# Target attention over a history: both halves of the next pair's scores ahead of the context, and one history transfer per group

## The chip, the cores and the metric

The kernel runs on one core of a Trainium2 chip. The metric is the device time of one execution in microseconds (us); the reference numbers are a median over runs. The engines are named as the profile names them: PE (TensorE matmuls) with PEld (its weight loads), DVE (VectorE), ACT (ScalarE), POOL (GpSimd) and SP (SyncE, which issues most DMAs; SPq is its queue).

## The reference, cut to what matters

For each of 2048 targets there is a history of 200 rows of 128 numbers and a mask of 200 flags. One query per target attends to its own history with four heads of 32.

```python
q = (target_item @ W_q).reshape(b, H, HD)            # b=2048, H=4, HD=32
k = (history_sequence @ W_k).reshape(b, S, H, HD)    # S=200
v = (history_sequence @ W_v).reshape(b, S, H, HD)
scores = jnp.einsum('bhd,bshd->bhs', q, k) / SCALE
scores = jnp.where(mask[:, None, :] == 0, NEG, scores)
attn = jax.nn.softmax(scores, axis=-1)
out = jnp.einsum('bhs,bshd->bhd', attn, v).reshape(b, A)
return out @ W_o
```

All data are float32. The history is 2048 x 200 x 128 x 4 bytes, 209.7 MB, and is read once. The kernel never forms k and v. It multiplies each target by W_q and W_k combined (four vectors `u` of 128 per target), takes the scores as `u` times the history, the context as the softmax weights times the history, and multiplies the context by W_v and W_o combined.

## The kernel before

**Tiling.** 16 targets make a *group*: their history fills one tile `hist[g % 6]` of 128 partitions (16 targets x 8) by 25 x 128 numbers. Two groups, i = 0 and 1, make a *pair* `p`; there are 64 pairs. Three pairs (96 targets) make a *round*, in which the targets are transposed (`transpose_target`), combined with the weights (`combine`) and the finished contexts are multiplied out (`outputs`). There are six history tiles, that is three pairs (RING = 3).

**One pair's way through the engines.** SP loads the history tile in two halves of 12 and 13 of its 25 slices (HALVES), and the mask. DVE transposes each half in 32 x 32 blocks into `blocks` (`turn`, four per pair; three `blocks` tiles exist). POOL spreads `u` into the padded weight tile `u_pad` (`spread`, 16 small copies) and turns the mask into `bias` (`mask_bias`). PE makes the scores of group 0 and of group 1 (`scores(p, 0)`, `scores(p, 1)`) into one PSUM bank `ps_s`. DVE adds the bias and takes the extreme (`maximum`), ACT takes the exponential (`exponent`), DVE divides and transposes (`turn_probs`, up to `probs_t`). PE places these weights (`place`, into `ps_p`), ACT expands them into `p_pad` with eight activations (`expand`), and PE multiplies them with the history (`context`, into two banks `ps_c`). ACT copies the context out (`finish`, to `ctx_sb`), PE transposes it while adding partial sums (`turn_context`, into `ps_y`), and ACT stores it in `ctx_t` (`copy_context`).

**Order.** Nothing is scheduled by a tool: each engine has its own program, written out by hand, and runs it in order, with semaphore waits between engines. The PE program is a sequence of `step(q)`, one for each pair, three to a turn of the loop. In step q the order is: `place(q)`, `scores(q+1, 0)`, wait for `expand(q)`, `turn_context` of pair q-1, `context(q)` of the first 12 slices of both groups, `scores(q+1, 1)`, `context(q)` of the other 13 slices. Where q is a multiple of three, `transpose_target` and `outputs` stand behind the first context half and `combine` behind `scores(q+1, 1)`. The DVE program for each pair p is `turn(p,0,0)`, `maximum(p-1)`, `turn(p,0,1)`, `turn_probs(p-1)`, `turn(p,1,0)`, `turn(p,1,1)`. The ACT program is `exponent(q)`, `finish(q-1)`, `expand(q)`, `copy_context(q-1)`, and in every third step the copies of the round (`copy_target`, `store`, `copy_combined`).

**When buffers come free.** A half of a history tile is loaded again once the context that reads this half for the pair three before has ended (L150). There is one `u_sb`, so that `copy_combined` waits until POOL has spread the last pair of the round before (L376). POOL's `mask_bias(p+2)` stands ahead of `spread(p+2)`, and waits for the mask that SP issued behind the first group's history of that pair.

**Start.** Behind the weight products PE makes 96 idle transposes (IDLE_TURNS), then the first scores.

## Time and profile before

| | |
|---|---|
| median of 3 runs | 766.93 us (765.03 to 769.29) |
| profiled execution, its own time | 765.87 us |
| span of the profiled execution | 764.1 us |
| PE / PEld / DVE busy | 76% / 59% / 68% of the span |
| ACT / POOL busy | 37% / 40% of the span |
| DMA queue of SP | 217.60 MB, 80.1% of 16 engines' span |
| mean DMA rate | 287 GB/s |

The span runs from the first to the last recorded instruction; the execution's own time is 1.8 us longer. A busy share is an average over the span, so no engine is at 100% although the work of one pair follows that of the other without a break. The rows quoted below carry, in order, the start in us, the duration in us, the engine, the line of the kernel, the operation with its tiles, the number of instructions merged into the row, and in brackets the idle time before it with what ended it.

### The profile page before, as it was taken

How to read it: one execution, taken by the hardware profiler on the slowest of the kernel's cores; microseconds unless marked ns; L12 is line 12 of the kernel's file. 1: busy time of each engine (PE TensorE's matmuls, PEld its weight loads, DVE VectorE, ACT ScalarE, POOL GpSimd, SP SyncE). 2: the span in 40 equal slices, each digit the busy share in tenths (PEclk: the TensorE clock that was granted, in tenths of full speed). 3: DMA queues.
4: the chain of work that ended last, by engine and by line, in shares of the span. 5: the costliest groups of instructions: out<-in, count | busy, mean ns of one | idle time of the engine just before them, and what ended most of it. 6: DMA issues, size and time to landing. Idle time of an engine off the chain costs nothing.

```text
span 764.1 us, 41709 instructions
## 1 busy us (share of the span) xinstructions
PE 578.2 (76%) x18665; PEld 449.7 (59%) x18665; DVE 520.7 (68%) x577; ACT 280.0 (37%) x909; POOL 305.7 (40%) x1123
## 2 busy tenths in 40 slices
PE   6877777777787777778777777878767777877776
PEld 5655665556566565556556555656656555655655
DVE  4475767776866767876776777686676777677660
ACT  2142334334433433433333433443343443343342
POOL 3624343453443344344344334344434434534420
PEclk9999999999999999999999999999999999999998
DMA  8578688788889788798978879898988979897940
GB/s 339 213 260 296 247 315 297 287 316 303 312 285 334 261 289 324 279 337 293 328 265 316 309 275 313 299 330 289 330 270 286 329 278 334 279 324 266 318 143 6
DMA packets 49808, 219.18 MB, mean 287 GB/s; under 512 B 5888, under 2 KB 16656, under 8 KB 49760
## 3 DMA queue, kind: packets, MB, share of 16 engines
q1 hardware_dynamic: 49056, 217.60, 80.1%
q0 software_dynamic: 704, 1.05, 0.4%
q8 instruction: 17, 0.28, 0.1%
q14 instruction: 31, 0.25, 0.1%
HBM read 217.58 MB, written 1.05 MB: 286 GB/s over the span
## 4 chain that ended last, share of the span: by engine, by line
PE 41%; ACT 17%; DVE 14%; DMA 10%; issue 9%; POOL 7%; SPq 1%; POOLq 0%; DVEq 0%; ACTq 0%
ACT p_pad L391 16%; PE ps_c L287 15%; PE ps_s L256 11%; DMA mask<-r_mask 10%; DVE blocks L456 8%; PE ps_p L270 7%; POOL u_pad L200 6%; PE ps_y L297 4%; DVE probs_t L480 3%; DVE weights L476 2%; PE ps_p L349 2%; POOL bias L204 1%; PE ps_y L304 1%; ACT probs L382 1%; DMA w_in<-L_rec_W_o 1%
## 5 line engine op out<-in xcount | busy, mean ns | idle before, releaser
L456 DVE STREAM_TRANSPOSE blocks<-hist 128x1536 f32<-128x1536 f32 (+1 forms) x256 | 454.4, 1812 | 6.4 <-DMA hist<-r_history_sequence 6.4
L200 POOL COPY u_pad<-u_sb 32x32 f32<-32x32 f32 x1024 | 233.6, 228 | 60.6
L287 PE MATMUL ps_c<-hist,p_pad 64*32 64x128 f32 x12800 | 221.4, 274 | 5.3 <-issue 4.8
L391 ACT ACTIVATE p_pad<-ps_p,own 128x200 f32<-128x200 f32 x512 | 169.7, 442 | 116.1 <-PE ps_p L270 116.1
L204 POOL TENSOR_SCALAR bias<-mask 128x200 f32<-128x200 int32 x64 | 56.4, 881 | 371.5 <-DMA mask<-r_mask 369.8
L256 PE MATMUL ps_s<-blocks,u_pad 128*32 128x200 f32 x4096 | 202.0, 338 | 0.0
L287 PEld LDWEIGHTS ps_c<-hist,p_pad 64*32 64x32 f32 x12800 | 185.3, 106 | 26.7 <-issue 19.4
L465 DVE CUSTOM_DVE_ANT_0 neg_score<-ps_s,bias 128x200 f32<-128x200 f32 x64 | 23.4, 366 | 198.9 <-PE ps_s L256 198.9
L256 PEld LDWEIGHTS ps_s<-blocks,u_pad 128*32 128x32 f32 x4096 | 121.0, 110 | 52.2 <-issue 8.8
L270 PE MATMUL ps_p<-probs_t,place_sel 128*64 128x112 f32 x1024 | 65.2, 271 | 82.8 <-DVE probs_t L480 82.8
L270 PEld LDWEIGHTS ps_p<-probs_t,place_sel 128*64 128x64 f32 x1024 | 51.3, 140 | 100.1 <-DVE probs_t L480 71.6
L297 PE MATMUL ps_y<-par_sel,ctx_sb 128*128 128x64 f32 x256 | 42.3, 288 | 84.5 <-ACT p_pad L391 84.0
L297 PEld LDWEIGHTS ps_y<-par_sel,ctx_sb 128*128 128x128 f32 x256 | 33.8, 192 | 109.1 <-issue 102.0
L382 ACT ACTIVATE probs<-neg_score,neg_max 128x200 f32<-128x200 f32 x64 | 29.6, 463 | 145.5 <-DVE neg_max L465 145.5
L406 ACT COPY ctx_t<-ps_y 128x128 f32<-128x128 f32 x64 | 25.4, 397 | 52.8 <-PE ps_y L297 52.8
L400 ACT COPY ctx_sb<-ps_c 128x128 f32<-128x128 f32 x128 | 27.6, 268 | 46.2 <-PE ps_c L287 46.1
L377 ACT COPY u_sb<-ps_u 128x384 f32<-128x384 f32 x22 | 10.5, 479 | 67.8 <-POOL u_pad L200 47.6
L480 DVE STREAM_TRANSPOSE probs_t<-weights 128x224 f32<-128x224 f32 x64 | 26.3, 411 | 2.9 <-DVE weights L476 0.2
L245 PE MATMUL ps_u<-x_t,w_qk 128*128 128x96 f32 x176 | 25.8, 291 | 2.8 <-issue 1.9
L245 PEld LDWEIGHTS ps_u<-x_t,w_qk 128*128 128x128 f32 x176 | 22.1, 197 | 9.8 <-issue 8.7
L304 PE MATMUL ps_y<-w_vo,ctx_t 128*96 128x128 f32 x176 | 23.1, 274 | 0.5 <-ACT ctx_t L406 0.5
L476 DVE TENSOR_SCALAR weights<-probs,inv_sum 128x200 f32<-128x200 f32 x64 | 20.9, 327 | 2.3
(42 smaller groups left out, 122.3 us busy)
## 6 DMA issues: line engine op xcount, KB each, us to landing
hist<-r_history_sequence SPq DMA_DIRECT2D x128, 832.0 KB, 7.9
hist<-r_history_sequence SPq DMA_DIRECT2D x128, 768.0 KB, 6.6
mask<-r_mask SPq DMA_DIRECT2D x64, 100.0 KB, 5.1
x_sb<-r_target_item SPq DMA_DIRECT2D x21, 48.0 KB, 9.0
out<-out_sb POOLq DMA_DIRECT2D x21, 48.0 KB, 4.5
w_in<-L_rec_W_q SPq DMA_DIRECT2D x1, 64.0 KB, 1.8
w_in<-L_rec_W_k SPq DMA_DIRECT2D x1, 64.0 KB, 2.2
w_in<-L_rec_W_v SPq DMA_DIRECT2D x1, 64.0 KB, 5.2
```

The source lines that it names most:

```text
L200: pool.tensor_copy(to, source[Q * c:Q * c + Q, a]).then_inc(u_pad_ready, 1)
L204: pool.tensor_scalar(bias[p % 2][:, :], mask_sb[p % RING][:, :], 0.0, BIG, ALU.is_equal, ALU.mult).then_inc(bias_ready, 1)
L245: mm = pe.matmul(ps_u[:, h * ROUND:(h + 1) * ROUND], w_qk[:, h, :], x_t[:, :], start=True, stop=True)
L256: mm = pe.matmul(ps_s[ring][Q * b:Q * b + Q, 0:S].rearrange("p (t j) -> p t j", j=J), u_pad[ring][:, i, b, c, :], blocks[slot][:, :, c, J ...
L270: mm = pe.matmul(ps_p[64 * alpha:64 * alpha + 64, 0:4 * TQ * 16].rearrange("p (q x i r) -> p x q i r", q=TQ, x=4, i=2)[:, x], place_sel[:, ...
L287: mm = pe.matmul(ps_c[alpha][at:at + Q, 0:D], p_pad[ring][rows, t + par, i, :], hist[2 * ring + i][rows, t + par, :], start=(t == 0), stop ...
L297: mm = pe.matmul(ps_y[:, 64 * alpha:64 * alpha + 64], ctx_sb[:, alpha, :], par_sel[:, :, :].rearrange("p i r -> p (i r)"), start=True, sto ...
L382: act.activation(probs[p % 2][:, :], neg_score[p % 2][:, :], ACT.Exp, bias=neg_max[:, 0:1], scale=-1.0, accum_out=row_sum[p % 2][:, 0:1]). ...
L391: op = act.activation(p_pad[p % RING][:, :, :, H * k:H * k + H].rearrange("p t i h -> p (t i) h"), source[:, k // 4], ACT.Copy, scale=own[ ...
L456: dve.transpose(blocks[g % BLOCKS][:, t0:t1].rearrange("p t c k -> p (t c k)"), hist[g % SLOTS][:, t0:t1, :].rearrange("p t d -> p (t d)") ...
L476: dve.tensor_scalar(weights[:, 0:S], probs[p % 2][:, :], inv_sum[:, 0:1], None, ALU.mult).then_inc(weighted, 1)
L480: dve.transpose(probs_t[:, :, :].rearrange("p q r -> p (q r)"), weights[:, :]).then_inc(probs_turned, 1)
```

## The change

Six things change together.

1. PE's step: both `scores(q+1, 0)` and `scores(q+1, 1)` stand right behind `place(q)`, ahead of the wait for `expand(q)`. The pieces of the round stand between the two scores, one for each step of the round: `transpose_target` where q mod 3 is 2, `combine` where it is 0, `outputs` where it is 1.
2. The context runs group by group, all 25 slices of group 0 and then of group 1, four slices side by side in the array in place of two slices of both groups. `ps_c` holds 2 x 128 columns, `finish` copies 256 columns for each bank, and `turn_context` makes four matmuls of 32 columns against `share_sel` in place of two of 64 against `par_sel`.
3. History is loaded in one transfer of 25 slices per group, once the context of the group six before has ended. DVE's two `turn`s of a group wait for that one transfer.
4. The mask of pair p+1 is issued behind the first history transfer of pair p. On POOL `spread(p+2)` stands ahead of `mask_bias(p+2)`, which waits for `maximum(p)` in place of `exponent(p)`.
5. `u_sb` is double, so that `copy_combined` waits for the spread of one round earlier. `outputs` writes into the `ps_u` bank.
6. IDLE_TURNS is 63 in place of 96.

```diff
-    IDLE_TURNS = 96
+    IDLE_TURNS = 63
...
-                    for h, (t0, t1) in enumerate(HALVES):
-
-                        wait(sp, ctx_done, 2 * (p - RING) + h + 1)
-                        sp.dma_start(
-                            hist[g % SLOTS][:, t0:t1, :], history_v[g * P:(g + 1) * P, t0:t1, :],
-                        ).then_inc(hist_loaded[g % SLOTS][h], 16)
...
+                    wait(sp, ctx_done, g - SLOTS + 1)
+                    sp.dma_start(hist[g % SLOTS][:, :, :],
+                                 history_v[g * P:(g + 1) * P, :, :]).then_inc(hist_loaded[g % SLOTS], 16)
+                    if i == 0 and p == 0:
+                        load_mask(0)
+                    if i == 0 and p + 1 < NP:
+                        load_mask(p + 1)
...
             for p in range(NP):
                 if p + 2 < NP:
-                    pool.wait_ge(exp_done, p + 1)
-                    pool.wait_ge(u_pad_ready, 16 * p + 32)
+                    pool.wait_ge(bias_ready, p + 2)
+                    spread(p + 2)
+                    pool.wait_ge(u_pad_ready, 16 * p + 48)
+
+                    pool.wait_ge(max_ready, p + 1)
                     mask_bias(p + 2)
-                    pool.wait_ge(bias_ready, p + 3)
-                    spread(p + 2)
...
-            def context(ring, half):
-                t0, t1 = HALVES[half]
-                for t in range(t0, t1, 2):
+            def context(ring, i):
+
+                for t in range(0, T, 4):
                     for alpha in range(2):
                         rows = slice(64 * alpha, 64 * alpha + 64)
-                        for i in range(2):
-                            for par in range(min(2, t1 - t)):
-                                at = Q * (2 * i + par)
-                                mm = pe.matmul(
-                                    ps_c[alpha][at:at + Q, 0:D],
-                                    p_pad[ring][rows, t + par, i, :],
-                                    hist[2 * ring + i][rows, t + par, :],
-                                    start=(t == 0), stop=(t + par + 2 >= T),
-                                )
+                        for x in range(min(4, T - t)):
+                            mm = pe.matmul(
+                                ps_c[alpha][Q * x:Q * x + Q, i * D:(i + 1) * D],
+                                p_pad[ring][rows, t + x, i, :],
+                                hist[2 * ring + i][rows, t + x, :],
+                                start=(t == 0), stop=(t + x + 4 >= T),
+                            )
                 mm.then_inc(ctx_done, 1)
 
             def turn_context():
                 for alpha in range(2):
-                    mm = pe.matmul(ps_y[:, 64 * alpha:64 * alpha + 64], ctx_sb[:, alpha, :],
-                                   par_sel[:, :, :].rearrange("p i r -> p (i r)"), start=True, stop=True)
+                    for i in range(2):
+                        at = 64 * alpha + Q * i
+                        mm = pe.matmul(ps_y[:, at:at + Q], ctx_sb[:, alpha, i, :], share_sel[:, :],
+                                       start=True, stop=True)
                 mm.then_inc(ctx_t_done, 1)
...
+            def step(q, ring, r, first=False, ahead=True, targets=True):
+
                 place(q)
                 if ahead:
-                    scores(q + 1, after, 0)
+                    scores(q + 1, (ring + 1) % RING, 0)
+                if targets and (ring == 2 or first):
+                    transpose_target(r + 2 if ring == 2 else 1)
+                if targets and ring == 0 and not first:
+                    combine(r + 1)
+                if ring == 1 and not (isinstance(r, int) and r == 0):
+                    outputs(q - 1)
+                if ahead:
+                    scores(q + 1, (ring + 1) % RING, 1)
                 pe.wait_ge(expanded, q + 1)
                 if not first:
                     pe.wait_ge(ctx_copied, 2 * q)
                     turn_context()
                 context(ring, 0)
...
-                wait(act, u_pad_ready, 16 * RING * r)
-                act.copy(u_sb[:, :, :], ps_u[:, 0:H * ROUND].rearrange("p (h n) -> p h n", h=H)).then_inc(u_copied, 1)
+                wait(act, u_pad_ready, 16 * RING * (r - 1))
+                act.copy(u_sb[r % 2][:, :, :], ps_u[:, 0:H * ROUND].rearrange("p (h n) -> p h n", h=H)).then_inc(u_copied, 1)
...
-                dve.wait_ge(hist_loaded[g % SLOTS][half], 16 * (g // SLOTS + 1))
+                dve.wait_ge(hist_loaded[g % SLOTS], 16 * (g // SLOTS + 1))
```

The first place is PE's program inside the loop, one step without and (after the change) one step with a piece of the round. `ps_s` are the scores, `ps_p` the placed weights, `ps_y` the turned context, `ps_c` the context; ISA and REGISTER_ALU rows set up loop counts. Before:

```order
L270 MATMUL ps_p<-probs_t,place_sel 64x7x16 x8
L250 ISA
L252 ISA
L256 MATMUL ps_s<-blocks,u_pad 32x200 x16
L316 REGISTER_ALU
L297 MATMUL ps_y<-par_sel,ctx_sb 128x64 x2
L287 MATMUL ps_c<-hist,p_pad 32x128 x48
L250 REGISTER_ALU
L256 MATMUL ps_s<-blocks,u_pad 32x200 x16
L287 MATMUL ps_c<-hist,p_pad 32x128 x52
```

After the change, in a step that holds `combine`:

```order
L273 MATMUL ps_p<-probs_t,place_sel 64x7x16 x8
L253 ISA
L255 ISA
L259 MATMUL ps_s<-blocks,u_pad 32x200 x16
L248 MATMUL ps_u<-x_t,w_qk 128x96 x4
L253 REGISTER_ALU
L259 MATMUL ps_s<-blocks,u_pad 32x200 x16
L326 REGISTER_ALU
L300 MATMUL ps_y<-share_sel,ctx_sb 128x32 x4
L288 MATMUL ps_c<-hist,p_pad 32x128 x100
```

The second scores moved from between the two context halves to ahead of the register row that carries the wait for the expanded weights; the piece of the round moved in between the two scores.

The second place is SP's queue in the steady part, over one pair. Before:

```order
L151 DMA hist<-r_history_sequence 128x1536 [waits ctx_done]
L151 DMA hist<-r_history_sequence 128x1664 [waits ctx_done]
L157 DMA mask<-r_mask 128x1x200 [waits bias_ready]
L151 DMA hist<-r_history_sequence 128x1536 [waits ctx_done]
L151 DMA hist<-r_history_sequence 128x1664 [waits ctx_done]
```

After the change:

```order
L157 DMA hist<-r_history_sequence 128x3200 [waits ctx_done]
L149 DMA mask<-r_mask 128x1x200 [waits bias_ready]
L157 DMA hist<-r_history_sequence 128x3200 [waits ctx_done]
```

Four history issues of 12 and 13 slices became two of 25, and the mask between them is that of the pair after.

## Rows read from the trace of the kernel before

**Rows 1.** The page: busy time by engine, DMA in all, and SP's DMA queue.

```profile
PE 578.2 (76%) x18665; PEld 449.7 (59%) x18665; DVE 520.7 (68%) x577; ACT 280.0 (37%) x909; POOL 305.7 (40%) x1123
...
DMA packets 49808, 219.18 MB, mean 287 GB/s; under 512 B 5888, under 2 KB 16656, under 8 KB 49760
...
q1 hardware_dynamic: 49056, 217.60, 80.1%
```

**Rows 2.** Waits: who waited for whom, us in total, times, longest.

```profile
DVE neg_score L465 <- PE ps_s L256: 198.9, 64, 11.3
...
PE ps_y L297 <- ACT p_pad L391: 84.0, 62, 2.8
...
ACT u_sb L377 <- POOL u_pad L200: 47.6, 14, 4.0
```

**Rows 3.** Timeline of a step without a round's piece, then the next placing.

```profile
402.92 1.59 PE L287 MATMUL ps_c<-hist,p_pad 64*32 64x128 f32 x96
...
404.45 1.56 PE L256 MATMUL ps_s<-blocks,u_pad 128*32 128x200 f32 x32
...
405.94 1.79 PE L287 MATMUL ps_c<-hist,p_pad 64*32 64x128 f32 x104
406.07 0.36 DVE L465 CUSTOM_DVE_ANT_0 neg_score<-ps_s,bias 128x200 f32<-128x200 f32 x1 [2.50 <-PE ps_s L256]
...
406.37 1.91 DVE L456 STREAM_TRANSPOSE blocks<-hist 128x1664 f32<-128x1664 f32 x1
...
409.05 5.19 DVE L456 STREAM_TRANSPOSE blocks<-hist 128x1536 f32<-128x1536 f32 x3
...
409.18 0.99 PE L270 MATMUL ps_p<-probs_t,place_sel 128*64 128x112 f32 x16 [1.44 <-DVE probs_t L480]
...
410.09 1.56 PE L256 MATMUL ps_s<-blocks,u_pad 128*32 128x200 f32 x32
410.21 2.65 ACT L391 ACTIVATE p_pad<-ps_p,own 128x200 f32<-128x200 f32 x8 [2.01 <-PE ps_p L270]
...
412.99 0.65 PE L297 MATMUL ps_y<-par_sel,ctx_sb 128*128 128x64 f32 x4 [1.34 <-ACT p_pad L391]
413.58 1.59 PE L287 MATMUL ps_c<-hist,p_pad 64*32 64x128 f32 x96
```

**Rows 4.** Timeline of the step after it, with the round's pieces.

```profile
415.24 1.04 PE L304 MATMUL ps_y<-w_vo,ctx_t 128*96 128x128 f32 x8
...
417.70 1.13 PE L245 MATMUL ps_u<-x_t,w_qk 128*128 128x96 f32 x8
...
419.78 0.48 ACT L377 COPY u_sb<-ps_u 128x384 f32<-128x384 f32 x1 [3.20 <-POOL u_pad L200]
...
421.84 0.99 PE L270 MATMUL ps_p<-probs_t,place_sel 128*64 128x112 f32 x16 [1.28 <-DVE probs_t L480]
```

**Rows 5.** Timeline: the first and the last of the 64 placings.

```profile
31.76 1.76 PE L270 MATMUL ps_p<-probs_t,place_sel 128*64 128x112 f32 x16 [3.18 <-DVE probs_t L480]
...
747.72 0.99 PE L270 MATMUL ps_p<-probs_t,place_sel 128*64 128x112 f32 x16
```

**Rows 6.** Timeline of the start: the idle transposes, the first two spreads, the first scores.

```profile
12.31 13.43 PE L349 MATMUL ps_p<-ident 128*128 128x128 f32 x96 [0.84 <-ACT w_vo L426]
...
18.85 9.17 POOL L200 COPY u_pad<-u_sb 32x32 f32<-32x32 f32 x32
...
25.67 2.91 PE L256 MATMUL ps_s<-blocks,u_pad 128*32 128x200 f32 x64
```

**Rows 7.** One history issue of 832 KB near 420.6 us: its issue, its landing.

```profile
L151 SPq DMA_DIRECT2D hist<-r_history_sequence x1: 328/328/328, 420.6 to 420.6; - x1
...
DMA to landing us min/median/max: 4.4/4.4/4.4
```

**Rows 8.** Stretches: length; busy PE, PEld, DVE, ACT, POOL; PE clock, DMA share, GB/s.

```profile
12.00:14.00 2.00, 1.69 (x8) 1.69 (x9) 1.74 (x2) 0.26 (x2) 0.00 (x0) 1.00 1.03 429
...
358.00:368.00 10.00, 7.18 (x280) 5.39 (x278) 7.36 (x10) 4.03 (x13) 4.73 (x18) 1.00 0.94 340
```

More of the change, by code:

```diff
@@ L72, in target_attention @@
         x_t = sb("x_t", [P, ROUND])
-        u_sb = sb("u_sb", [P, H, ROUND])
+        u_sb = [sb(f"u_sb{n}", [P, H, ROUND]) for n in range(2)]
         w_in = sb("w_in", [P, 4, P])
@@ L223, in _ @@
                     pool.dma_start(out[r * ROUND:(r + 1) * ROUND, :], out_sb[:, :]).then_inc(out_stored, 16)
-            for r in range((NP - 1) // RING - 1, NR):
+            for r in range(NR - 2, NR):
                 pool.wait_ge(y_copied, r + 1)
@@ L318, in step @@
                 context(ring, 0)
-                if ring == 0 and combines:
-                    transpose_target(r + 1)
-                if ring == 0 and not first:
-                    outputs(q)
-                if ahead:
-                    scores(q + 1, after, 1)
-                if ring == 0 and combines:
-                    combine(r + 1)
                 context(ring, 1)
+                if first:
+                    combine(1)
             transpose_target(0)
@@ L337, in _ @@
             combine(0)
[L338 removed]
+            pe.wait_ge(sel_ready, 2)
             pe.wait_ge(vo_loaded, 32)
```

72 lines of the change are left out of this document (36 added, 36 removed).

## The prediction, made before the changed kernel ran

> **What bounds the kernel now.** I read the page first: no engine and no queue is full, PE is busy 76% of the span and SP's DMA queue 80.1% [rows 1]. So the limit is a chain that passes through several engines, and the question is who waits. The waits answer it [rows 2]: DVE's `maximum` waits for PE's scores in all 64 pairs, 198.9 us in sum; PE waits for ACT's `expand` 62 times, 84.0 us. PE's placing in turn waits for DVE [rows 3]. Each engine waits for the next one once a pair, which is the picture of one closed loop.
>
> The timeline of a plain step gives the loop its length [rows 3]. Placing starts at 409.18, `expand` at 410.21, and PE sits idle from the end of `scores(q+1,0)` until `turn_context` at 412.99; the context starts at 413.58, 4.40 us after the placing. In the step before, the context starts at 402.92, the second scores at 404.45 (1.53 later), `maximum` at 406.07 (1.62 later), the transposition of the next half at 406.37, and the next placing, behind that half and `turn_probs`, at 409.18. That is 1.53 + 4.73 = 6.26 us, with the 4.40 us a step of 10.66 us. The third step of a round is longer, from 409.18 to 421.84 = 12.66 us [rows 3, 4]: the pieces of the round stand inside the loop, and `copy_combined` waits 3.20 us for POOL's spread, which waits for a late mask; behind this copy in ACT's order stands the exponential.
>
> Over the kernel, the 63 steps between the first and the last placing take 747.72 - 31.76 = 715.96 us, 11.36 us each [rows 5]. Ahead of them lie 31.76 us and behind them 764.1 - 747.72 = 16.38 us.
>
> **What the change does to a step.** *PE's chain.* The loop ran through `expand`, then the context, then the second scores. Now the second scores run while ACT expands. From the placing, the first scores start after 0.91 us and each takes about 1.52 us (the step from 404.45 to the second context at 405.94, 1.49, and 1.56 in the row) [rows 3]; both are done after 0.91 + 3.04 = 3.95. `expand` ends at 410.21 + 2.65, 3.68 us after the placing, so it is just covered: if this cover fell short, PE would pay what is missing, at most the 2.65. Then `turn_context`: two matmuls in four passes of 0.59 us before [rows 3]. Four matmuls need eight passes with 128-column weights; the nearest rows are eight passes in 1.13 us (96 columns) and 1.04 us (128 columns) [rows 4]. From below the cost is 0.59 (only the columns count, which are as many as before), from above 1.13; I take 1.05, since the number of passes and weight loads is that of the second rows. Then the context. Before, 12 slices of two groups were six turns of the array in 1.53 us, and 13 slices seven turns, the last half empty, in 1.79 [rows 3]. Now each group has seven turns (6 x 4 + 1 slices), so 2 x 1.79 = 3.58 against 3.32, +0.26 (lower bound: equal, if the lone slice overlaps with what follows). Sum of a plain PE step: 3.95 + 1.05 + 3.58 = 8.6 us. The round's pieces add 1.04, 1.13 and about 0.3 us with gaps of about 0.1 each, (2.47 + 0.3) / 3 = 0.9 a step. PE alone would therefore go at **9.5 us a step**, at 9.3 with the lower bounds.
>
> At this place a rule speaks against the change. The Trainium skill (TensorEngine Tiling (Array Packing), Instruction Overhead) says that a matmul over very few columns takes as long as one over 60. By it four matmuls of 32 columns cost twice the two of 64, 1.2 to 1.3 us in place of my 1.05, and a step 0.2 us more. No row here has a 32-column moving operand.
>
> *DVE.* Its work for a pair is 5.19 us for three transpositions, 0.30 for `maximum` (406.07 to 406.37), and 2.81 for the fourth transposition and `turn_probs` (406.37 to 409.18): 8.3 us [rows 3], below PE. From the scores to the next placing DVE needs the same 4.73 us less 1.62, that is 3.1 us; PE is meanwhile in `turn_context` and the context for 4.6 us, so this way is hidden.
>
> *ACT.* `finish` copies 256 columns for each bank, inside the 0.9 us in which PE places. Cost zero; without this cover some 0.2 us (its 128-column pair is shorter than the 0.48 us of the 384-column row [rows 4] by little). The exponential now follows `copy_context` in ACT's order, which waits for `turn_context`; its result is wanted about 2.1 us after `maximum` starts, since DVE transposes a half in between, and ACT is free at about 5.4 us, 1.4 us after the scores. Zero, and about 0.5 in the steps that hold `copy_combined`.
>
> *POOL and mask.* The mask comes a pair earlier and the spread no longer stands behind it; `copy_combined` waits for a spread one round older. The 47.6 us of waits [rows 2] go, and with them what made the 12.66 us step longer than its pieces.
>
> *History: the wait that comes next.* A group's transfer starts only when the whole context of the group six before is done, and DVE may start only when all of it has landed. Follow this loop: load of (q+3,0), issued when `context(q,0)` ends; landing; `turn` 1.7 (a third of 5.19); `maximum(q+2)` 0.3; the second `turn` and `turn_probs(q+2)` 2.81; placing and first scores of pair q+3 against DVE's two turns of the other group (3.6), then the second scores 1.56, together 5.2 (`combine` or `outputs` fits in here nearly free); `turn_context` 1.05; `context(q+2,0)` 1.79; which releases the slot for (q+5,0). It spans two steps. The landing: a piece of 832 KB, with the shortest landing of its stretch and so with little queued ahead, landed after 4.4 us [rows 7]; the other 768 KB (0.786 MB) add 1.8 us at 429 GB/s, 2.3 us at 340 GB/s [rows 8], so 6.2 to 6.7; I take 6.5. Sum: 6.5 + 1.7 + 0.3 + 2.81 + 5.2 + 1.05 + 1.79 + 0.1 (semaphores) = 19.45 us, **9.7 us a step**, above PE's 9.5.
>
> *The DMA queue.* 217.60 MB / 64 = 3.40 MB a step [rows 1]. At 340 GB/s, the rate of a well filled stretch with share 0.94, that takes 10.0 us; scaled to a full share, 362 GB/s, 9.4; at the 429 GB/s of the start, with the other engines nearly idle, 7.9 [rows 8]. I take 9.4 to 10.0, since the steady stretches are the nearest.
>
> The Trainium skill (DMA: Bandwidth & Descriptors, Where 436 GB/s comes from) puts a core's share of HBM at about 358 GB/s and the ports' ceiling at 435. By the first the step is 9.5 us, by the second 7.8; the start's 429 shows that the first is no hard limit for this lone core.
>
> Three limits of 9.5, 9.7 and 9.4 to 10.0 lie so close that each disturbs the other: when the queue is nearly full, a transfer stands behind the one before it. I take **9.85 us a step**.
>
> **Start and end.** 33 fewer idle transposes of 13.43 / 96 = 0.14 us bring the first scores 4.6 us forward, from 25.67 to 21.1 [rows 6]. This needs the first `u_pad`: it was begun at 18.85, behind two masks, and one spread is 9.17 / 2 = 4.6 us; POOL now begins it when `u_sb` is there, before the masks, so it is ready in time. If not, the 4.6 us are lost. At the end the turned context and the longer context add about 0.5: 16.9.
>
> **Sum.** 31.76 - 4.6 + 63 x 9.85 + 16.9 = 664.6 us of span, plus the 1.8 us around it (765.87 against 764.1) = 666 us. The profiled execution lies 1.1 us under the median of 766.93, so no correction beyond that; I say **666 us**, 13% less.
>
> **The rivals.**
> - *PE is the bound (chance 0.25).* Transfers run nearer 429 than 340 GB/s once the queue always holds something; landing is then 6.2 us or less and the step PE's 9.3 to 9.5. For it: the 429 row [rows 8], and that the share of 80.1% leaves a fifth of the time idle [rows 1]. Against: no steady 10 us stretch shows it. Time: 27.2 + 63 x 9.4 + 16.9 + 1.8 = 638 us.
> - *The DMA queue is the bound, more slowly than its share says (0.17).* Nothing but contention with the now busier engines would do this. At 330 GB/s the step is 10.3 us: 695 us.
> - *The second scores do not leave the loop (0.04).* If ACT's order holds the exponential back behind `turn_context` and then the round's copies in every step, the chain stays near today's 10.66 without the mask's part: 27.2 + 63 x 10.66 + 18.7 = 717 us.
> - *Slower than before (0.03).* One transfer in place of two halves lands late every time, since it starts a half later and DVE cannot begin on its first half. The place is DVE's first `turn` of a pair; each us of landing costs 0.5 us a step, and it decides against the change from a landing of 6.5 + 2 x (11.36 - 9.7) = 9.8 us on, or if the queue sustains less than 3.40 MB / 11.36 us = 299 GB/s. The mean of before is 287, but with a share of 80.1% [rows 1], so 358 at a full share, which speaks against. At 287 GB/s the step is 11.85: 792 us.
>
> **How the numbers follow.** The likeliest case, a step of 9.6 to 10.1 us bounded by the slot loop and the queue together, has 0.51 and runs from 651 to 682 us. To hold 8 in 10 the range takes in PE's case from a step of 9.35 on (635 us) and the queue's case up to a step of 10.35 (698 us). Faster by over 0.5%: 0.51 + 0.25 + 0.17 + 0.04, less a little, 0.96; within 0.5% (about what a measurement of this kernel can tell from no change) 0.01; slower 0.03.
>
> **What would show it.** Right: PE's wait for `p_pad` at `turn_context` falls from 84.0 us to under 15; `turn_context` takes about 1.05 us and the two contexts 3.6 together; DVE's `turn` waits for the history DMA, 0.3 to 1 us a step (before, this wait was in no row of weight); the wait of `u_sb` for POOL is gone; DMA share 0.93 or more over the middle with 340 to 360 GB/s; first placing near 27 us. Wrong: `turn` never waits for DMA (then PE bounds), a landing of one group above 9 us when the queue was empty, or a `maximum` that still waits 3 us for scores in each pair.

## The result, and the profile after

The changed kernel takes **671.42 us** (median of 4 runs, 666.03 to 675.83), the kernel before on the same chip 766.72 us (4 runs, 765.03 to 769.29): a ratio of 0.8751, with a 95% interval of 0.8682 to 0.882. The prediction was 666 us, range 635 to 698. The profiled execution took 666.03 us, with a span of 664.2 us. Lines of its page that answer to [rows 1], with two parts more, the queues that bring instructions and the chain that ended last:

```profile
PE 596.5 (90%) x18888; PEld 485.2 (73%) x18888; DVE 520.3 (78%) x578; ACT 285.1 (43%) x909; POOL 306.5 (46%) x1122
...
q1 hardware_dynamic: 30624, 217.59, 84.6%
...
q8 instruction: 17, 0.28, 0.2%
...
PE 39%; DMA 28%; DVE 20%; issue 10%; ACT 1%; SPq 1%; DVEq 0%; POOLq 0%; POOL 0%
...
L300 PE MATMUL ps_y<-share_sel,ctx_sb 128*128 128x32 f32 x512 | 69.8, 280 | 2.8 <-ACT p_pad L396 2.8
```

PE's busy time is 3% longer than before (596.5 against 578.2 us) and DVE's the same, the time is 12.5% shorter: the same work stands closer together. PE's wait for `p_pad`, 84.0 us in [rows 2], is 2.8 us (last line). The waits show who took its place (columns as in [rows 2]):

```profile
DVE blocks L465 <- DMA hist<-r_history_sequence: 104.7, 64, 6.8
...
PE ps_p L273 <- DVE probs_t L489: 32.7, 39, 3.2
```

DVE, which waited 198.9 us for scores, now waits 104.7 us for history, once a pair (8.7 us for scores), and no wait of `u_sb` for POOL is left. The first and the last placing, against [rows 5]:

```profile
28.20 1.76 PE L273 MATMUL ps_p<-probs_t,place_sel 128*64 128x112 f32 x16 [3.17 <-DVE probs_t L489]
...
646.51 0.99 PE L273 MATMUL ps_p<-probs_t,place_sel 128*64 128x112 f32 x16
```

63 steps take 646.51 - 28.20 = 618.3 us, 9.81 us each, and 664.2 - 646.51 = 17.7 us lie behind. The timeline of one step in the middle, in which the piece between the two scores is `transpose_target`, against [rows 3]:

```profile
404.17 0.99 PE L273 MATMUL ps_p<-probs_t,place_sel 128*64 128x112 f32 x16 [0.85 <-DVE probs_t L489]
405.08 1.56 PE L259 MATMUL ps_s<-blocks,u_pad 128*32 128x200 f32 x32
405.20 2.66 ACT L396 ACTIVATE p_pad<-ps_p,own 128x200 f32<-128x200 f32 x8 [1.20 <-PE ps_p L273]
...
407.54 1.56 PE L259 MATMUL ps_s<-blocks,u_pad 128*32 128x200 f32 x32 [0.66 <-DVE blocks L465]
408.67 1.78 DVE L465 STREAM_TRANSPOSE blocks<-hist 128x1536 f32<-128x1536 f32 x1 [1.18 <-DMA hist<-r_history_sequence]
409.03 1.08 PE L300 MATMUL ps_y<-share_sel,ctx_sb 128*128 128x32 f32 x8
...
410.04 3.29 PE L288 MATMUL ps_c<-hist,p_pad 64*32 64x128 f32 x200
...
413.44 0.99 PE L273 MATMUL ps_p<-probs_t,place_sel 128*64 128x112 f32 x16
```

`expand` ends at 407.86, well before PE reaches `turn_context` at 409.03: the wait that cost PE most is covered by the scores. DVE's transposition at 408.67 had waited 1.18 us for its history. The chain that ended last, over four steps (two turns of the loop that is left), cut to its main pieces:

```profile
392.63 6.66 DMA hist<-r_history_sequence
...
401.02 0.33 DVE neg_score L474
...
405.62 1.88 DVE blocks L465
...
407.54 1.56 PE ps_s L259 x32
409.10 1.01 PE ps_y L300 x8
410.11 1.71 PE ps_c L288 x103
...
411.83 6.62 DMA hist<-r_history_sequence
...
429.27 1.71 PE ps_c L288 x105
...
430.99 6.95 DMA hist<-r_history_sequence
```

From one history load to the one that it releases, 392.63 to 411.83 and on to 430.99, are 19.20 and 19.16 us for two steps. It passes landing, DVE, the second scores, `turn_context` and the context of group 0: the loop that the prediction follows under "History", called the slot loop from here on, because it is closed by a history tile (a slot) that comes free. The stretch from 200 to 300 us (columns as in [rows 8]) shows that the DMA queue is not full:

```profile
200.00:300.00 100.00, 92.21 (x3023) 74.66 (x3010) 83.86 (x95) 45.67 (x146) 46.90 (x173) 1.00 0.91 350
```

### The profile page after: what moved, and what is told of

It is laid out like the page before. It is cut to its first block, busy times and chain, and to the rows that moved or that the text cites. A ratio compares the mean times of both kernels' runs of the same rounds, so it can differ in the third digit from the quotient of the medians.

```text
span 664.2 us, 42026 instructions
## 1 busy us (share of the span) xinstructions
PE 596.5 (90%) x18888; PEld 485.2 (73%) x18888; DVE 520.3 (78%) x578; ACT 285.1 (43%) x909; POOL 306.5 (46%) x1122
## 3 DMA queue, kind: packets, MB, share of 16 engines
q0 software_dynamic: 704, 1.05, 0.4%
HBM read 217.58 MB, written 1.05 MB: 329 GB/s over the span
## 4 chain that ended last, share of the span: by engine, by line
PE 39%; DMA 28%; DVE 20%; issue 10%; ACT 1%; SPq 1%; DVEq 0%; POOLq 0%; POOL 0%
DMA hist<-r_history_sequence 28%; DVE blocks L465 15%; PE ps_s L259 14%; PE ps_c L288 10%; PE ps_y L300 5%; PE ps_p L273 4%; PE ps_u L248 2%; DVE weights L485 2%; PE ps_u L307 2%; DVE neg_score L474 2%; PE ps_p L353 1%; DVE probs_t L489 1%; DMA w_in<-L_rec_W_o 1%; ACT p_pad L396 0%; DVE inv_sum L483 0%
## 5 line engine op out<-in xcount | busy, mean ns | idle before, releaser
L465 DVE STREAM_TRANSPOSE blocks<-hist 128x1536 f32<-128x1536 f32 (+1 forms) x256 | 461.4, 1822 | 104.7 <-DMA hist<-r_history_sequence 104.7
L288 PE MATMUL ps_c<-hist,p_pad 64*32 64x128 f32 x12800 | 214.3, 274 | 4.8 <-issue 4.8
L259 PE MATMUL ps_s<-blocks,u_pad 128*32 128x200 f32 x4096 | 201.0, 337 | 14.9 <-DVE blocks L465 12.8
L288 PEld LDWEIGHTS ps_c<-hist,p_pad 64*32 64x32 f32 x12800 | 195.7, 106 | 9.3 <-issue 6.6
L405 ACT COPY ctx_sb<-ps_c 128x256 f32<-128x256 f32 x128 | 41.4, 375 | 119.4 <-PE ps_c L288 119.4
L300 PEld LDWEIGHTS ps_y<-share_sel,ctx_sb 128*128 128x128 f32 x512 | 62.8, 193 | 22.6 <-issue 19.6
L300 PE MATMUL ps_y<-share_sel,ctx_sb 128*128 128x32 f32 x512 | 69.8, 280 | 2.8 <-ACT p_pad L396 2.8
L474 DVE CUSTOM_DVE_ANT_0 neg_score<-ps_s,bias 128x200 f32<-128x200 f32 x64 | 21.1, 330 | 8.7 <-PE ps_s L259 8.7
L307 PEld LDWEIGHTS ps_u<-w_vo,ctx_t 128*96 128x96 f32 x176 | 19.8, 162 | 7.1 <-issue 6.6
L307 PE MATMUL ps_u<-w_vo,ctx_t 128*96 128x128 f32 x176 | 24.5, 282 | 0.5 <-ACT ctx_t L411 0.5
```

Source lines behind the costliest of these rows:

```text
L259: mm = pe.matmul(ps_s[ring][Q * b:Q * b + Q, 0:S].rearrange("p (t j) -> p t j", j=J), u_pad[ring][:, i, b, c, :], blocks[slot][:, :, c, J ...
L288: mm = pe.matmul(ps_c[alpha][Q * x:Q * x + Q, i * D:(i + 1) * D], p_pad[ring][rows, t + x, i, :], hist[2 * ring + i][rows, t + x, :], star ...
L300: mm = pe.matmul(ps_y[:, at:at + Q], ctx_sb[:, alpha, i, :], share_sel[:, :], start=True, stop=True)
L307: mm = pe.matmul(ps_u[0:ROUND, H * ROUND:H * ROUND + D], ctx_t[:, h, :], w_vo[:, h, :], start=(h == 0), stop=(h == H - 1))
L405: act.copy(ctx_sb[:, alpha, :, :], ps_c[alpha][:, 0:2 * D].rearrange("p (i d) -> p i d", i=2)).then_inc(ctx_copied, 1)
L465: dve.transpose(blocks[g % BLOCKS][:, t0:t1].rearrange("p t c k -> p (t c k)"), hist[g % SLOTS][:, t0:t1, :].rearrange("p t d -> p (t d)") ...
```

## The experiments

The theory: three parts each take something out of a loop (the scores out of PE's, the late mask out of POOL's and ACT's, the round's pieces out of the place where they stood together), and what then bounds is the slot loop, which the single transfer lengthens. The rivals: PE itself bounds, or the queue does. All 12 kernels are told, in three groups. Each is timed against the kernel before on its own chip (762.86 to 766.34 us there). The diffs are against the changed kernel unless said otherwise.

### Which part brings the gain

**Second scores alone ahead**, in the kernel before:

```diff
                     scores(q + 1, after, 0)
+                    scores(q + 1, after, 1)
                 pe.wait_ge(expanded, q + 1)
...
-                if ahead:
-                    scores(q + 1, after, 1)
```

> The kernel before with one edit: both scores of the next pair stand right behind the placing, everything else as before (half transfers, context by halves of both groups, late masks, one u_sb). If the serial loop through the expansion, the context and the second scores was the cost, the step falls from 11.36 us to about 10.0 (PE's own order gives 8.8, the history and the late mask give back a part): 31.8 + 63 x 10.0 + 18 = about 680 us. If the regrouped context and the single transfers bring the gain, it stays at 755 to 767 us.

Measured: 742.92 us (740.72 to 746.16), ratio 0.9698 (0.9623 to 0.9772): 23 us in place of 86, a miss. The waits and the chain of this kernel say why:

```profile
POOL bias L204 <- DMA mask<-r_mask: 307.9, 53, 14.4
...
PE ps_s L256 <- POOL u_pad L200: 51.1, 33, 2.4
```
```profile
393.27 8.01 DMA mask<-r_mask
...
418.07 6.89 DMA mask<-r_mask
...
430.70 5.56 PE ps_s L256 x64
```

POOL waits for the mask, spreads late, and PE's scores wait for `u_pad`. Steps in the middle last some 8.5, 9.9 and 14 us; the third holds the round's pieces and `copy_combined`. The part that looked like an accessory is what lets the first part count (`scores_pool96` below adds it to this kernel).

The clock has a share in this miss too. The stretch with the last row of the chain (columns as in [rows 8]):

```profile
430.00:440.00 10.00, 9.30 (x180) 6.50 (x181) 5.02 (x5) 2.15 (x7) 5.07 (x20) 0.69 0.68 257
```

The 64 rows of scores take 5.56 us in place of 2 x 1.49 = 2.98, at a granted clock of 0.69, so partly at its lower level (1.2 GHz); PE had just waited 1.62 us for `probs_t` and 2.16 us for `u_pad`. Over the run the clock is 0.927, against 0.988 in the kernel before, and PE is busy 597.2 us, against 562.0 us in `scores_pool96`, which makes the same matmuls at 0.986. Up to 35 us of this kernel's time can thus be the clock; how much of them lies on the chain is not separated.

**Second scores put back**, all else changed:

```diff
-                if ahead:
-                    scores(q + 1, (ring + 1) % RING, 1)
                 pe.wait_ge(expanded, q + 1)
...
                 context(ring, 0)
+                if ahead:
+                    scores(q + 1, (ring + 1) % RING, 1)
                 context(ring, 1)
```

> The changed kernel with one edit taken back: the second scores stand between the contexts of group 0 and group 1 again. Serial loop theory: 10.66 of before plus 0.4 for the longer turn_context and 0.1 for the context is 11.2 us a step, with the round's pieces now under the expansion: 27.2 + 63 x 11.2 + 18.8 = about 752 us. The rival, that transfers and POOL's order bring most of the gain: below 700 us.

Measured: 769.03 us (764.81 to 772.07, 10 runs), ratio 1.0036 (1.0003 to 1.007): 17 us above the theory's 752, and far from the rival's 700. Its waits:

```profile
DVE neg_score L474 <- PE ps_s L259: 211.7, 64, 5.2
...
PE ps_p L273 <- DVE probs_t L489: 98.9, 64, 3.2
```

The old loop is back, and DVE waits for scores, not for history. With it closed, all the other parts together are worth nothing, gains and costs taken together.

**Old order of mask and spread on POOL and SP**, and `copy_combined` waiting for the last spread as before:

```diff
-                    if i == 0 and p == 0:
-                        load_mask(0)
-                    if i == 0 and p + 1 < NP:
-                        load_mask(p + 1)
+                    if i == 0:
+                        load_mask(p)
...
+                    pool.wait_ge(exp_done, p + 1)
+                    pool.wait_ge(u_pad_ready, 16 * p + 32)
+                    mask_bias(p + 2)
+                    pool.wait_ge(bias_ready, p + 3)
                     spread(p + 2)
...
-                wait(act, u_pad_ready, 16 * RING * (r - 1))
+                wait(act, u_pad_ready, 16 * RING * r)
```

> The changed kernel with the parts on POOL taken back: the mask of pair p behind the history of pair p, mask_bias(p+2) behind the exponential of p and ahead of spread(p+2), and copy_combined waiting for the spread of its own round. My theory: the spread ends about 9 us after the placing, the copy and the exponential queued behind it come 2 us late in each third step: 671 + 15 to 40, about 695 us. Rival from the run with the scores alone (743 us): the late mask is most of what it lacked, 720 to 740 us.

Measured: 713.0 us (709.57 to 715.98), ratio 0.9339 (0.9297 to 0.9381): 42 us more than the changed kernel, between the theory's 686 to 711 us and the rival's 720 to 740. The wait that came back:

```profile
POOL bias L204 <- DMA mask<-r_mask: 304.0, 60, 10.1
```

Alone the scores bring 23 us, without POOL's part the rest brings 50 us (762.86 on this chip less 713.0), all together 95 us. The two loops lie side by side, so each edit is worth less until the other is made.

### What bounds the changed kernel

**History in two halves again**, with the new order and the new context:

```diff
                     wait(sp, ctx_done, g - SLOTS + 1)
-                    sp.dma_start(hist[g % SLOTS][:, :, :],
-                                 history_v[g * P:(g + 1) * P, :, :]).then_inc(hist_loaded[g % SLOTS], 16)
+                    for h, (t0, t1) in enumerate(HALVES):
+                        sp.dma_start(hist[g % SLOTS][:, t0:t1, :],
+                                     history_v[g * P:(g + 1) * P, t0:t1, :]).then_inc(hist_loaded[g % SLOTS][h], 16)
...
-                dve.wait_ge(hist_loaded[g % SLOTS], 16 * (g // SLOTS + 1))
+                dve.wait_ge(hist_loaded[g % SLOTS][half], 16 * (g // SLOTS + 1))
```

> The changed kernel with each group's history in two transfers of 12 and 13 slices again, both issued when the group six before is done, and DVE waiting for each by itself. Slot loop theory (landing of a whole group, then both turns, lies in a loop of 19.2 us over two steps): the first turn starts on the first half, the loop gets 1.6 to 2 us shorter and PE (about 9.0) or the queue is next: a step of 9.2 to 9.4, about 635 us, range 622 to 650. Queue bandwidth theory: the bytes are the same and the packets twice as many, so 668 us or more.

Measured: **630.95 us** (628.15 to 633.91), ratio 0.8213 (0.8144 to 0.8281), as expected. It is the fastest kernel of this study, 6% under the changed one. A wait, the stretch of 200 to 300 us, and the chain of one step and the next placing:

```profile
DVE blocks L466 <- DMA hist<-r_history_sequence: 40.3, 68, 4.3
```
```profile
200.00:300.00 100.00, 99.67 (x3256) 81.38 (x3248) 91.97 (x101) 49.30 (x161) 50.53 (x186) 1.00 0.98 383
```
```profile
407.26 0.92 PE ps_p L274 x16
408.18 1.49 PE ps_s L260 x32
409.67 1.04 PE ps_u L308 x8
410.71 1.49 PE ps_s L260 x32
412.20 1.01 PE ps_y L301 x8
413.21 3.22 PE ps_c L289 x193
...
416.54 0.99 PE ps_p L274 x16
```

PE is now busy throughout, and the chain stays on it from step to step (86% of the span on the page). Its steps repeat as 9.19, 9.35 and 8.36 us, 8.97 on average: that is PE's own length. And the queue carries 383 GB/s at share 0.98 where it carried 350 at 0.91: in the changed kernel it was no limit, in this one it has little left.

**A wider `turn_context`** (each of the four matmuls writes its 32 columns eight times, and the copies are not read):

```diff
-                        mm = pe.matmul(ps_y[:, at:at + Q], ctx_sb[:, alpha, i, :], share_sel[:, :],
-                                       start=True, stop=True)
+                        mm = pe.matmul(ps_y[:, at:at + 8 * Q].rearrange("p (k r) -> p k r", r=Q), ctx_sb[:, alpha, i, :],
+                                       share_sel[:, :].unsqueeze(1).broadcast_to([P, 8, Q]), start=True, stop=True)
```

> The changed kernel with the same four matmuls in turn_context, each 256 columns wide in place of 32 (the sums repeated eight times, the last ones read as before), so that PE has about 0.9 us more work in each pair with not one instruction more. Slot loop theory: once in a loop over two steps, 0.45 us a step, 671 + 28 = about 699 us. PE as the bound: 728 us. Queue bandwidth: under 10 us more. Instructions fetched stay at 0.28 MB.

Measured: 700.34 us (695.08 to 704.49, 6 runs), ratio 0.9181 (0.9118 to 0.9245), where the slot loop gave 699. The matmuls, and DVE's wait for history:

```profile
404.53 1.99 PE L300 MATMUL ps_y<-share_sel,ctx_sb 128*128 128x256 f32 x8
```
```profile
DVE blocks L465 <- DMA hist<-r_history_sequence: 131.4, 65, 6.8
```

0.91 us more in each step made the step 0.45 us longer (10.26 against 9.81), half of it. A loop that passes this place once in two steps must do that; were PE the bound, it would be all of it, and were the queue the bound, none. PE is not far behind: its own length would be 8.97 + 0.91 = 9.88 us here, and behind the fifth step the steps last 10.18 us. This and `halves` settle it: the slot loop bounds.

**The same test, tried twice before**, with the four matmuls made twice, and with two extra matmuls of 384 columns ahead of them (neither changes the result that is stored):

```diff
-                for alpha in range(2):
+                for alpha in (0, 1, 0, 1):
```

> The changed kernel with turn_context's four matmuls issued twice, about 1.0 us more work for PE in each pair, ahead of the context. Slot loop theory: it lies once in a loop over two steps, so 0.5 us a step: about 32 us more, 703 us. PE as the bound: 1.0 us a step, 734 us. Queue bandwidth as the bound: under 10 us more.

```diff
+                    for _ in range(2):
+                        pe.matmul(ps_y[:, P:4 * P], ident[:, :], w_vo[:, 0:3, :].rearrange("p h n -> p (h n)"),
+                                  start=True, stop=True)
                     turn_context()
```

> The changed kernel with two extra matmuls of 384 columns ahead of turn_context in every step but the first (they write columns of its PSUM bank that nobody reads), about 0.8 us of PE work in each pair with only 6 more matmuls in the loop body, where turn_twice had 12. Slot loop theory: once in a loop over two steps, 0.4 us a step, 671 + 25 = about 696 us, and no stop at the loop's turn. PE as the bound: 721 us. If a stop of some 7.6 us at each turn of the loop comes here too, about 830 us: then any growth of the body does it.

Measured: 820.48 us (815.06 to 831.38), ratio 1.0694 (1.0587 to 1.0801), and 837.83 us (835.89 to 850.34), ratio 1.0967 (1.0922 to 1.1012). Both are over 85 us above either theory's figure, and each shows the same thing; here the first placing of a turn of the loop in the twice-turned kernel, and the queue that brings PE's instructions:

```profile
421.29 1.76 PE L273 MATMUL ps_p<-probs_t,place_sel 128*64 128x112 f32 x16 [7.64 <-issue]
```
```profile
q8 instruction: 98, 1.61, 0.9%
```

PE stands still for 7.64 us at the head of the loop, waiting for nothing that the profile shows but its own issue, and q8 moves 1.61 MB in place of 0.28. The second kernel stops for 7.77 us and moves the same 1.61 MB. So neither kernel decides between the theories. The third group follows this up.

**Eight history slots, so that a load is released two steps earlier.** Four pairs of slots don't fit a loop of three steps, so PE's program is written out straight:

```diff
-    SLOTS = 2 * RING
+    SLOTS = 8
...
-            with pe.Fori(0, LOOPS) as r:
-                step(3 * r + 2, 2, r)
-                step(3 * r + 3, 0, r + 1)
-                step(3 * r + 4, 1, r + 1)
+            for n in range(2, NP - 2):
+                step(n, n % 3, n // 3, n % 4)
```

> The changed kernel with eight history tiles in place of six, so that a group's transfer waits for the group eight before; PE's steps are written out without a loop, since the tile numbers repeat only after 12 steps. Slot loop theory: the loop of 19.2 us now spans three steps, so PE is next at 9.0 us a step: 27 + 63 x 9.1 + 19 = about 620 us, and DVE's waits for history fall from 105 us to under 30. Queue bandwidth theory: 660 us or more. If fetching straight-line code holds PE up, long issue waits show it.

Measured: 782.13 us (777.09 to 789.28), ratio 1.0224 (1.0171 to 1.0276), far over the 620 us of the slot loop theory. DVE's wait for history is gone from the large waits, but PE's issue took its place (its scores wait another 29.3 us so):

```profile
PEld ps_c L288 <- issue: 86.1, 62, 4.2
PE ps_c L288 <- issue: 69.3, 59, 3.9
```

So it decides nothing about the slot loop. As these waits read, PE works through straight code faster than the code is brought; that no loop is there rules out the loop's head as the only place.

### Where the loop's body lies

**The changed kernel with 96 idle transposes**, as before the change:

```diff
-    IDLE_TURNS = 63
+    IDLE_TURNS = 96
```

> The changed kernel with 96 idle turns in place of 63. If IDLE_TURNS is only a start-up time: 33 x 0.14 = 4.6 us more, 676 us, instructions fetched once (0.28 MB). If the place of the loop body in the program decides (here 132 instructions later): the body of 1784 instructions is fetched anew at each turn, 800 us or more.

Measured: 773.28 us (768.25 to 782.07), ratio 1.0108 (1.0013 to 1.0202); the profiled execution is the one of 782.07. Three stops in a row at the head of the loop, and the stretch of 395 to 407.2 us around the second:

```profile
338.24 1.76 PE L273 MATMUL ps_p<-probs_t,place_sel 128*64 128x112 f32 x16 [7.89 <-issue]
...
407.36 1.76 PE L273 MATMUL ps_p<-probs_t,place_sel 128*64 128x112 f32 x16 [7.83 <-issue]
...
478.26 1.76 PE L273 MATMUL ps_p<-probs_t,place_sel 128*64 128x112 f32 x16 [7.92 <-issue]
```
```profile
395.00:407.20 12.20, 4.52 (x216) 3.99 (x208) 8.16 (x9) 1.70 (x6) 7.58 (x29) 0.85 0.96 369
```

The loop is instruction for instruction that of the changed kernel; only what stands ahead of it differs, by 33 matmuls. That costs 102 us. q8 moves 1.61 MB in 98 packets, as in the two kernels above. Around the stop the DMA engines have a share of 0.96, nearly all of it history, and q8's time is counted on the same 16 engines; that this crowding makes the stop so long is argued, and no run takes the history away to show it.

The stops stand some 70 us apart, which is six steps, so two turns of the loop. There are nine of them in the 20 turns (LOOPS), and between one and the next q8 moves nine packets (from 338.24 to 407.36 us as from 407.36 to 478.26): the body is brought anew in every second turn, which is why the time stays under the 800 us of a body brought in each. From 125.47 to 688.22 us, eight such pairs of turns take 70.3 us each, against 6 x 9.69 = 58.1 in the changed kernel. That is 12.2 us for a stop of 7.8, and 9 x 12.2 = 110 us of the 116 by which this execution is longer than the profiled one of the changed kernel. The rest of each 12.2 us goes to shorter issue waits ahead of context matmuls, 40.1 us in all (4.8 in the changed kernel), and to the clock, which is 0.931 over the run in place of 0.991, and 0.85 in the stretch above, in which PE stands still; a part of all this is covered by PE's slack against the slot loop. I have no run that tells these shares apart.

**Scores and POOL's part without the rest**, that is the first experiment with `mask_bias`, `spread`, the mask's issue and the double `u_sb` as in the changed kernel, and 63 idle transposes; then the same with 96. Against that first experiment:

```diff
-    IDLE_TURNS = 96
+    IDLE_TURNS = 63
...
+                    if i == 0 and p == 0:
+                        load_mask(0)
+                    if i == 0 and p + 1 < NP:
+                        load_mask(p + 1)
...
-                    mask_bias(p + 2)
-                    pool.wait_ge(bias_ready, p + 3)
+                    pool.wait_ge(bias_ready, p + 2)
                     spread(p + 2)
+                    pool.wait_ge(u_pad_ready, 16 * p + 48)
+                    pool.wait_ge(max_ready, p + 1)
+                    mask_bias(p + 2)
```

> The kernel before with the scores ahead and the parts on POOL (early masks, spread ahead of the mask, two u_sb, 63 idle turns), but with half transfers and the context by halves of both groups as before. If the late masks held back the run with the scores alone, PE bounds: 0.91 + 2.98 + 0.59 + 3.1 + 0.8 of pieces is 8.4 a step, DVE's 8.3 beside it: about 9.0 a step, 31.8 - 4.6 + 567 + 18 = 612 us, range 600 to 640. If the grouped context and single transfers are what brings the gain, above 671 us.

> scores_pool with 96 idle turns in place of 63 and nothing else changed: PE's loop body is the same 1760 instructions, but begins 132 instructions later in the program. In scores_pool 3.06 MB of instructions were fetched (0.28 MB in the kernel before, with the same body) and PE stopped in every step. If where the body lies decides whether it stays in PE's instruction buffer, the fetch falls back to about 0.28 MB and PE bounds at 8.4 to 9.0 us a step: 590 to 625 us. If the order of the work itself held PE up, it stays above 900 us.

Measured: 932.09 us (926.45 to 1023.75), ratio 1.2186 (1.2126 to 1.2245), and 681.16 us (678.67 to 684.7), ratio 0.8931 (0.8861 to 0.9002). The profiled execution of the first ran at a granted clock of 0.55 and is the 1023.75, so only its count of instructions is used: 3.06 MB on q8, against 0.28 in the second. The same 33 matmuls, now the other way round, are worth 251 us, at a granted clock of 0.85 in the three shorter runs of the first and 0.98 to 0.99 in the second. Beside the first experiment (742.92 us) the second shows that the parts on POOL and the double `u_sb` take off another 62 us, the clock's share in it included, and that with the scores they bring 84 us in the kernel before, without a grouped context and without a single transfer.

The second misses its 590 to 625 us by 56: with the round's pieces all in one step, the steps go 11.3, 8.5 and 9.8 us. Spreading them over the round is worth something too, since `copy_combined` stands ahead of the exponential on ACT:

```profile
DVE inv_sum L479 <- ACT probs L387: 55.5, 22, 3.9
```

**The context in its old form**, with halves and all the rest of the change, and 65 idle transposes, meant to put the loop where it was:

```diff
-            def context(ring, i):
-
-                for t in range(0, T, 4):
+            def context(ring, half):
+                t0, t1 = HALVES[half]
+                for t in range(t0, t1, 2):
...
-    IDLE_TURNS = 63
+    IDLE_TURNS = 65
```

> The changed kernel with the context and the transfers of before (by halves of both groups, turn_context in two matmuls, a half of a tile loaded again when its context half has ended), and 65 idle turns, which put the loop body at the same start as in the changed kernel (1601 instructions in), 24 shorter. PE's own step is 0.91 + 2.98 + 0.59 + 3.1 + 0.8 = 8.4 us, DVE's 8.3, the queue's 3.40 MB at 380 GB/s 8.9. If the queue is next after the transfers in halves, 8.9 to 9.1 us a step: 615 to 632 us, beside halves' 631. If the grouped context has a worth of its own by freeing a whole tile earlier, above 645 us. If nothing but PE counts: 590 us.

Measured: 972.16 us (961.16 to 979.09, 6 runs), ratio 1.2667 (1.2593 to 1.2742), a miss again through the loop's head:

```profile
PE ps_p L276 <- issue: 206.0, 20, 12.8
```

19 of these are stops of 9.8 to 12.8 us, one at each of the 19 branches back to the loop's head, 10.8 us each on average; the twentieth is short. So what the grouped context is worth stays open. In `scores_only` the old form takes 0.59 us of `turn_context` and 3.05 us of context, against 1.01 and 3.22 in `halves`: PE's step would be 0.6 us shorter with it, if the loop could be placed.

The positions can be counted in the programs. A matmul of these kernels is four instructions (two weight loads, two multiplications). The straight kernel has 2 x 18,888 of them on its page, and its q8 moved 2.42 MB: 64 bytes each. The body is 432 + 9 matmuls and some 20 register instructions; the place where the loop begins is counted from the matmuls ahead of it alone. The last column counts how often PE stops for issue at the loop's head, which 20 turns reach 19 times by the branch back:

| kernel | loop begins at PE's instruction | length | q8 | stops |
|---|---|---|---|---|
| before, `scores_only`, `scores_pool96` | 1157 | 1760 | 17 packets, 0.28 MB | 0 |
| after, `halves`, `scores_back`, `old_pool` | 1601 | 1784 | 17, 0.28 | 0 |
| `wide_turn` | 1601 | 1784 | 16, 0.26 | 0 |
| `longer_turn` | 1609 | 1808 | 98, 1.61 | 9 |
| `turn_twice` | 1617 | 1832 | 98, 1.61 | 9 |
| `idle96` | 1733 | 1784 | 98, 1.61 | 9 |
| `old_context` | 1601 | 1760 | 187, 3.06 | 19 |
| `scores_pool` | 1025 | 1760 | 187, 3.06 | 19 |

A packet is 1.61 MB / 98 = 16.4 KB, 256 instructions; the body is 7 of them. Against the 17 packets of a program that is read once, 81 more are nine for each of the nine stops, and 170 more are nine for each of 19, less one: a stop brings the body whole and two packets beside it, either in every second turn of the loop or in every one. The same length is fetched once at 1601 and again in every second turn at 1733; the same start is free with 1784 instructions and dear with 1760. I found no rule of start, end or length that fits all rows, so the condition stays open; that it hangs on position is shown by `idle96` and `scores_pool96`, which change nothing else in the program (the 33 matmuls also move the loop's start in time by 4.6 us; no run has the one without the other).

## Why the prediction held, point by point

- *The slot loop, 19.45 us.* Right, 19.20 and 19.16 us. Term by term from the chain: landing 6.62 (6.5), the context of group 0 1.71 (1.79), `turn_context` 1.01 (1.05), `maximum` 0.33 (0.3). `wide_turn` and `halves` show that it is this loop.
- *The step, 9.85 us.* 9.81, but not by the addition that I made. I put 0.15 on the loop for a full queue. Yet the steps behind the fifth last 9.69 us on average, near the loop's own 9.6, and the first five last 12.1, 10.8, 10.6, 10.3 and 12.8 us, 8.1 us too long together. In this stretch PE's idle times that end in issue add to 6.2 us, the longest 2.08, and q8 moves 11 of its 17 packets; between 90 and 630 us it moves none. These five steps are the two ahead of the loop and its first turn, so code that is read for the first time. That this and the 0.15 came out alike was luck.
- *PE alone, 9.5 us.* Mis-sized: 8.97. The term is the context, 3.58 predicted and 3.22 measured, under the lower bound of 3.32. I had counted turns of the array and read row lengths that overlap with what follows; 200 matmul rows in 3.22 us are 16.1 ns each, and 96 in 1.53 us of [rows 3] are 15.9, so it fits the number of matmuls, and the lone slice shows no turn of its own. The scores (2 x 1.49) and the round's pieces give the rest. The 9.3 us that I gave for PE at its lower bounds was also added up wrongly: 0.59 for `turn_context` and 3.32 for the context give 3.95 + 0.59 + 3.32 + 0.9 = 8.8, and 8.97 lies above that. The rival "PE bounds" was thus priced too high: its time would have been 28.2 + 63 x 9.0 + 17.7 + 1.8 = 615 us, outside my range, not 638. `halves` reaches 631 because its first six steps last 11.7 us on average.
- *`turn_context`, 1.05 us.* Right, 1.01. By the floor of 60 columns that the Trainium skill (TensorEngine Tiling (Array Packing), Instruction Overhead) states, my estimate was 1.2 to 1.3. The measured 1.01 is under that. That short passes save little is borne out, and beyond 60 columns: eight of 32 columns take 1.01 us, eight of 96 take 1.06 in the chain of `halves`, and eight of 256 take 1.92 in that of `wide_turn`.
- *The queue, 9.4 to 10.0 us a step.* Wrong in size. The changed kernel does 350 GB/s, within the forecast 340 to 360, at share 0.91, a little under the 0.93 that I asked for, but because it is held back: `halves` does 383. At that rate a step is 8.9 us, and the rival of a queue at 330 GB/s had nothing for it. I had set the 429 GB/s aside as those of a start with idle engines, which was misread: in that stretch PE is busy 1.69 and DVE 1.74 of 2.00 us [rows 8].
- *The single transfer.* It was priced inside the loop (landing 6.5, against 4.4 for a half) and never set against its alternative. It is the one part that is shown to cost: 671 - 631 = 40 us.
- *Mask, spread, double `u_sb`.* Right that the waits go; 42 us in `old_pool`.
- *DVE's wait for history, 0.3 to 1 us a step.* It is 104.7 / 64 = 1.6 us, since DVE's 8.3 us leave 1.5 of 9.81 and all of it gathers at this one place.
- *Idle transposes, 4.6 us.* The mechanism held (the first scores start at 22.12 us, 3.6 us earlier, and the first placing at 28.2, not 27.2). The edit's real weight was nowhere in the sum, which put the fetching of code at nothing without a word on it: with 96 of them the kernel takes 773 us and the change brings nothing. That the 63 lay in a good place was luck for the forecast.

## What to carry to other kernels

When a wait goes, write the next loop down with its landing times: here the sum of the slot loop gave the step within 0.2 us, and the same sum shows that a transfer in two pieces, on the first of which work can begin, beats one large one. Try an edit against the full set of others, since the scores were worth 23 us alone and 98 us as the last step, and read the granted clock beside each time, since a part of such a difference can be the clock's. And look at the instruction queue of every kernel with a long PE loop: if it moves more than the program's size, shift the loop by idle matmuls before judging any other edit.

## What the runs showed of the hardware

A PE loop of some 1,800 instructions is brought once (17 packets), or again in every second of its turns (98), or in every turn (187). Where it is brought again PE stands still at its head: 7.1 to 8.3 us in `idle96`, `turn_twice` and `longer_turn`, 10.8 on average and 12.8 at most in `old_context`. It cost 102 us (773.28 against 671.42) and 251 us (932.09 against 681.16) for 33 matmuls ahead of the loop. Straight code of the same matmuls makes PE wait as well, 69.3 us before its context matmuls alone.

The Trainium skill (Runtime: NRT & Kernel Launch, Instruction fetch mechanics) says that instructions come in blocks of 16 KiB, that crossing into the next is mostly hidden, and that a taken branch out of the fetched window forces a fetch. The runs agree with the size (16.4 KB a packet). They agree with the branch's cost where the loop is brought again (7.83 us at its head), while in the changed kernel the branch back over 1784 instructions, 7 blocks, brings none in 20 turns. "Mostly hidden" they do not bear out: the straight code has no branch, and PE waits 69.3 us in it.

The queue sustained 383 GB/s over 100 us on this lone core, beside a PE that was busy 99.67% of that time.

Behind a standstill of PE its granted clock was at the lower level for a while: 0.69 from 430 to 440 us of `scores_only`, behind waits of 1.62 and 2.16 us, and 64 rows of scores then take 5.56 us in place of 2.98.
